# A selective scan with a gated MLP and a binary MLP on one core: loads of u and B on 64 rows, the second binary relu on ScalarE, one gating operation, last products in four steps

## The chip, the core and the metric

The kernel runs on one core of a Trainium2 chip. A core has five engines, each with an instruction stream of its own: PE (matrix products), DVE (vector), ACT (scalar, with function tables), POOL (general vector) and SP, which here only issues DMAs. They meet through semaphores. The metric is the device time of one execution in microseconds; lower is better.

## What is computed

Input x is 8 batches of 512 tokens of 128 numbers. It is normalised per token (layernorm), and the result `xn` goes through two blocks whose outputs are added to x:

```python
# block 1: E = 256, N = 64
xp = rmsnorm(xn) @ in_proj_W;  x_z, z = xp[..., :E], xp[..., E:]
xc = silu(depthwise_conv4(x_z) + conv_b)
dt = clip(softplus(xc @ dt_W + dt_b), 0.001, 0.1);  Bp = xc @ B_W;  Cp = xc @ C_W;  A = -exp(A_log)
def step(h, ins):                       # 512 steps in order, h is (8, 256, 64)
    h = exp(dt_t[..., None] * A) * h + dt_t[..., None] * B_t[:, None, :] * x_t[..., None]
    return h, einsum('ben,bn->be', h, C_t)
y = y * silu(z);  x = xn + y @ out_proj_W
x = x + (silu(n2 @ gate_W) * (n2 @ up_W)) @ down_W      # n2 = rmsnorm(x)
# block 2: weights of +1 and -1, layers 256 -> 512 -> 512 -> 128
h = s0 * conn(k0, [xn, -xn]);  h = relu(h) * 2;  h = s1 * conn(k1, h);  h = relu(h) * 2;  h = s2 * conn(k2, h)
```

## The kernel before

The work has two phases. In the first (up to about 175 us) the batches go one by one through norm, projection, convolution, softplus and the products for B and C. dt is written to `dt_stage` in DRAM in f32. u = dt times x is split into NP = 3 bf16 parts that add up to the f32 value and goes to `u_stage`, B likewise to `b_stage`. silu(z) stays in SBUF as `silu_z`. The core processes even and odd batches as two halves (bb) of the 128 partitions: a partition of the state is one pair (n, bb), a row of the state has Q = 4 batch pairs times E = 256 columns.

The second phase is the scan, 512 steps of t. Q is halved: two quarters are "self" (`state` in SBUF, decayed by POOL, added by DVE) and two are "acc" (held in PSUM, decayed by DVE, added by PE into PSUM). Per step:
- ACT turns a loaded dt row, broadcast over 64 partitions for each bb, into `decay` = exp(-A dt) (L1010, two steps at once) and copies the acc half to `state` (L1030);
- POOL multiplies `decay` and `state` for the two self quarters (L593, `decayed`);
- DVE multiplies the acc half in PSUM by `decay` (L1221) and adds POOL's product and PE's self input (L1232, two operations);
- PE forms the outer products of u and B: for acc L743, for self L750, each with contraction over 64 rows of `moving` (u parts) and `b_rows` (B parts); L798 contracts the state of three steps before (LAG) with C.

The rows of a product are the pairs of one u part and one B part of one batch. There are 3 x 3 x 4 = 36 for each of two hq, and they lie on the partitions `product_rows(hq)`, every third from 10 + hq on; the rest of the 128 partitions is zeroed once, by POOL and DVE (L578, L579, L1202, L1203). A chunk is TC = 16 steps. Its four loads are L194 (`load_u`, each u row broadcast to three partitions) and L201 (`load_b`), once for each hq.

SP issues, in the order of its program: dt loads (L392, two of 512 KB every two steps, one for each bb, each onto every second partition, as soon as the state of five slots before is done; `decay` has NDEC = 6 slots), the chunk loads half a body ahead, token loads and stores of results. All DMAs of the kernel are in one queue.

A body is STEPS = 32 steps (two chunks). The program has 3 bodies, then a loop of 4 rounds with 3 bodies each, then the last. Between its scan instructions each engine handles one group of 256 tokens of everything behind the scan (out projection, MLPs), by a table of step numbers K_...: at step k of a body come the group's entries k, k + 32 and k - 32, so that K_LAST = 33 means step 1 of the body after. The entries that matter here: K_GATED (DVE, steps 7 and 8, L1298: y times silu(z), two operations of 128 columns each), K_H2 (PE, the second binary layer, L883, steps 14 to 21 and 24 to 31), K_H2_RELU (DVE, its relus, L1345: 22 and 23 for the first half in two operations, 32 for the second), K_HID (33), K_LAST and LAST_STEPS (PE, L897, 12 products of the last binary layer and of down_W, shared over five steps 33 to 37) and K_XN_T (PE, transposes of the next group at step 2, L816). PE works in its own order, so what stands in front of the next L743 delays it, and L743 stands between two L1221 of DVE. After the scan the last group runs alone (`finish_last`).

## Time and profile before

| | us |
|---|---|
| runs of the kernel before | 1122.29, 1122.53, 1107.89 (median 1122.29) |
| the profiled execution, its own time | 1115.98 |
| its span from first to last instruction | 1114.2 |
| granted TensorE clock, mean | 0.96 |

A row of the page that groups instructions gives: line, engine, operation, out<-in with sizes, count, then busy time and mean ns of one, then the idle time of the engine before them and what ended it. In a view of stretches the columns are: stretch and length, busy time of each engine with the number of instructions, the granted clock, the mean busy share of the 16 DMA engines (DMA share) and GB/s. In a view of waits: who waited for what, us in total, times, the longest. In a timeline: start, duration, engine, line, operation, names, and in brackets idle time before it with its releaser.

### The profile page before, as it was taken

What the parts mean: (1) busy time and instruction counts of PE and PEld (TensorE: products, weight loads), DVE (VectorE), ACT (ScalarE), POOL (GpSimd) and SP (SyncE); (2) the same over time, 40 slices, a digit from 0 to 9 for tenths busy, and PEclk for the clock granted to TensorE, in tenths of its full rate; (3) what the DMA queues carried; (4) which work ended last, traced back from release to release, by engine and by line L of the source; (5) the groups of instructions that cost most, each with busy time, mean ns of one, the idle gap of its engine ahead of it and who ended that gap; (6) DMA issues with size and microseconds to landing.
All of it is one profiled execution on the core that took longest, in us unless ns stands there. A gap on an engine that the chain in (4) does not pass through costs nothing.

```text
span 1114.2 us, 27718 instructions
## 1 busy us (share of the span) xinstructions
PE 967.9 (87%) x8006; PEld 426.6 (38%) x8006; DVE 935.2 (84%) x2131; ACT 908.7 (82%) x1093; POOL 847.9 (76%) x1216
## 2 busy tenths in 40 slices
PE   5998883668999999998999887899998899999897
PEld 3555540113333343433333332334343334343436
DVE  5677663799989999997998887899998899999983
ACT  1666776789999999997988887899997899998980
POOL 6555513789888889887888786898887788988880
PEclk9999996789999999999999999899999899999999
...
GB/s 139 81 136 180 136 200 298 345 327 355 351 343 334 345 355 350 345 344 268 356 341 332 319 328 318 271 351 352 353 349 333 280 366 343 339 356 340 335 148 10
DMA packets 76758, 327.39 MB, mean 294 GB/s; under 512 B 13472, under 2 KB 32800, under 8 KB 41504
## 3 DMA queue, kind: packets, MB, share of 16 engines
...
HBM read 303.24 MB, written 22.02 MB: 292 GB/s over the span
## 4 chain that ended last, share of the span: by engine, by line
DVE 27%; PE 25%; POOL 19%; issue 16%; DMA 5%; ACT 5%; SPq 2%; DVEq 1%; POOLq 0%; ACTq 0%
POOL decayed L593 13%; DVE ps L1221 9%; PE ps L798 8%; DVE state L1232 7%; PE ps L743 5%; PE ps L897 5%; DMA decay<-dt_stage 4%; PE ps L883 3%; DVE h L1336 2%; ACT state L1030 2%; DVE h L1345 1%; DVE soft L1147 1%; POOL soft L543 1%; SPq L392 1%; POOL u_rest L553 1%
## 5 line engine op out<-in xcount | busy, mean ns | idle before, releaser
L593 POOL TENSOR_TENSOR decayed<-decay,state 128x256 f32<-128x256 f32 x1024 | 725.5, 733 | 169.1 <-DVE state L1232 125.4
L1010 ACT ACTIVATE decay<-decay,a_col 128x2048 f32<-128x2048 f32 x256 | 512.7, 2003 | 46.3 <-DMA decay<-dt_stage 36.5
L1232 DVE TENSOR_TENSOR state<-decayed,ps 128x256 f32<-128x256 f32 x1024 | 403.1, 417 | 55.4 <-POOL decayed L593 40.0
L1221 DVE TENSOR_TENSOR ps<-decay,ps 128x512 f32<-128x512 f32 x512 | 352.6, 689 | 40.5 <-ACT state L1030 17.2
L1030 ACT COPY state<-ps 128x512 f32<-128x512 f32 x512 | 288.9, 582 | 64.6 <-issue 43.2
L798 PE MATMUL ps<-state,c_cols 128*32 128x256 f32 x4096 | 338.2, 403 | 0.1
L743 PE MATMUL ps<-moving,b_rows 64*128 64x256 bf16 x1024 | 204.3, 281 | 100.5 <-DVE ps L1221 96.3
L750 PE MATMUL ps<-moving,b_rows 64*128 64x256 bf16 x1024 | 205.4, 282 | 12.0 <-DMA b_rows<-b_stage 12.0
L883 PE MATMUL ps<-h,w 128*128 128x256 f32 x512 | 175.8, 429 | 1.0 <-DVE h L1336 0.8
L743 PEld LDWEIGHTS ps<-moving,b_rows 64*128 64x128 bf16 x1024 | 58.4, 94 | 274.0 <-DVE ps L1221 172.3
L798 PEld LDWEIGHTS ps<-state,c_cols 128*32 128x32 f32 x4096 | 82.0, 109 | 113.4 <-issue 101.3
L883 PEld LDWEIGHTS ps<-h,w 128*128 128x128 f32 x512 | 79.7, 191 | 92.3 <-issue 89.1
L750 PEld LDWEIGHTS ps<-moving,b_rows 64*128 64x128 bf16 x1024 | 57.3, 95 | 12.4 <-DMA moving<-u_stage 12.3
L652 PE MATMUL ps<-n_feat,w_tap 128*128 128x512 f32 x128 | 59.3, 617 | 1.0 <-ACT n_feat L917 1.0
L897 PE MATMUL ps<-w,h 128*128 128x128 f32 x256 | 48.0, 305 | 1.0 <-DVE h L1345 1.0
L897 PEld LDWEIGHTS ps<-w,h 128*128 128x128 f32 x256 | 35.4, 196 | 26.2 <-issue 24.3
L848 PE MATMUL ps<-xn_feat,w 128*128 128x256 f32 x128 | 44.2, 429 | 0.2 <-DVE result L1354 0.2
L679 PE MATMUL ps<-w_dt,xc_feat 128*128 128x256 f32 x128 | 35.9, 439 | 9.0 <-ACT xc_feat L927 9.0
L679 PEld LDWEIGHTS ps<-w_dt,xc_feat 128*128 128x128 f32 x128 | 32.1, 328 | 12.9 <-ACT xc_feat L927 10.9
L652 PEld LDWEIGHTS ps<-n_feat,w_tap 128*128 128x128 f32 x128 | 24.8, 199 | 30.1 <-issue 30.1
L1147 DVE TENSOR_TENSOR soft<-soft 128x1024 f32<-128x1024 f32 x8 | 20.8, 2602 | 16.3 <-POOL soft L543 16.3
L543 POOL TENSOR_TENSOR soft<-soft 128x1024 f32<-128x1024 f32 x7 | 17.2, 2453 | 20.6 <-DVE soft L1136 20.6
...
## 6 DMA issues: line engine op xcount, KB each, us to landing
decay<-dt_stage SPq DMA_DIRECT2D x512, 512.0 KB, 6.6
moving<-u_stage SPq DMA_DIRECT2D x64, 288.0 KB
...
b_rows<-b_stage SPq DMA_DIRECT2D x64, 144.0 KB
dt_stage<-dt_tok SPq DMA_DIRECT2D x8, 512.0 KB, 3.1
u_stage<-u_parts SPq DMA_DIRECT2D x8, 512.0 KB, 2.8
x_tok<-in_L_attn_x_dram SPq DMA_DIRECT2D x4, 512.0 KB, 3.5
...
```

What stands on the lines that cost most here:

```text
L593: nc.gpsimd.tensor_tensor(decayed[:, p], decay[:, dec_slot(m, k), p, k % TS, :], state[:, (k - 1) % RING, p * E:(p + 1) * E], ALU.mult).th ...
L652: m = nc.tensor.matmul(ps[:, XC + h, :], w_tap[:, k, h * P:(h + 1) * P], n_feat[:, bass.ds(n, 1), k:k + T].rearrange("d o t -> d (o t)"), ...
L679: m = nc.tensor.matmul(ps[:, DTT + j // 2, (j % 2) * E:(j % 2 + 1) * E], xc_feat[:, bb, h, j:T:NJ], w_dt[:, h, :], start=(h == 0), stop=(h ...
L743: return nc.tensor.matmul(ps[:, acc_bank(m, k), p * E:(p + 1) * E], b_rows[rows(1), cb, p, kk, :], moving[rows(1), cb, kk, :], start=False ...
L750: return nc.tensor.matmul(ps[:, SELFP + k % 2, p * E:(p + 1) * E], b_rows[rows(0), cb, p, kk, :], moving[rows(0), cb, kk, :], start=True, ...
L798: m = nc.tensor.matmul(ps[q * 32:(q + 1) * 32, YP, 0:E], c_cols[:, cb, q, kk * 2 * TC:(kk + 1) * 2 * TC], state[:, k % RING, q * E:(q + 1) ...
L883: m = nc.tensor.matmul(ps[:, FB, c * GTOK:(c + 1) * GTOK], w1[:, n, f:f + P], h1[:, n, :], start=(n == 0), stop=(n == H1 // P - 1))
L897: m = nc.tensor.matmul(ps[:, FB, j * P:(j + 1) * P], terms[c][0][:, j * P:(j + 1) * P], terms[c][1], start=(c == 0), stop=(c == len(terms) ...
L1010: nc.scalar.activation(pair, pair, ACT.Exp, scale=a_col[:, 2:3]).then_inc(decay_ready, 1)
L1030: nc.scalar.copy(state[:, k % RING, SELF:QE], ps[:, acc_bank(m, k), :]).then_inc(acc_copied, 1)
L1221: nc.vector.tensor_tensor(ps[:, acc_bank(m, k), :].rearrange("p (q e) -> p q e", q=HQ), decay[:, dec_slot(m, k), HQ:Q, k % TS, :], ps[:, a ...
L1232: nc.vector.tensor_tensor(state[:, k % RING, p * E:(p + 1) * E], decayed[:, p], ps[:, SELFP + k % 2, p * E:(p + 1) * E], ALU.add).then_inc ...
```

## The change

It has five parts.
1. u and B get a fourth part of zeros (NS = 4), so there are 4 x 4 x 4 = 64 rows for each hq, and they lie on every second partition. The zero planes of `u_stage` and `b_stage` are written once by 24 stores of SP, from a part of `moving` that POOL has zeroed. The zeroing of the whole of `moving` goes.
2. The relu of the second binary layer moves from DVE to ACT, at steps 23 and 32, in one operation of 512 columns each.
3. `silu_z` is laid out by chunks, so that gating is one DVE operation of 512 columns at step 8.
4. K_LAST is 34 and LAST_STEPS is 4: the 12 products take steps 34 to 37, three a step.
5. A wait for the zero stores stands before the first chunk loads.

```diff
--- before.py
+++ after.py
-    ROWS = NP * NP * HALF
-    RSTEP = 3
-    RFIRST = HROW + RSTEP - 1 - RSTEP * (ROWS // 2)
-    assert RFIRST > 0 and HROW + HQ - 1 + RSTEP * (ROWS // 2) <= P
+    NS = NP + 1
+    ROWS = NS * NS * HALF
+    assert HQ * ROWS == P
...
-    u_stage = nc.dram_tensor("u_stage", (HQ, HQ, 2, NP, T, E), BF16, kind="Internal").ap()
+    u_stage = nc.dram_tensor("u_stage", (HQ, HQ, 2, NS, T, E), BF16, kind="Internal").ap()
     dt_stage = nc.dram_tensor("dt_stage", (2, T // TS, Q, TS, E), F32, kind="Internal").ap()
-    b_stage = nc.dram_tensor("b_stage", (HQ, HQ, 2, NP, NP, T, 2 * N), BF16, kind="Internal").ap()
+    b_stage = nc.dram_tensor("b_stage", (HQ, HQ, 2, NS, NS, T, 2 * N), BF16, kind="Internal").ap()
...
-        silu_z = sb("silu_z", [P, EH, B, T])
+        silu_z = sb("silu_z", [P, EH, NC, B, TC])
...
-            first = RFIRST - 2 + hq
-            return slice(first, first + RSTEP * (ROWS - 1) + 1, RSTEP)
+            return slice(hq, P, HQ)
 
         def load_u(sp, t, cb, hq):
 
             sp.dma_start(moving[product_rows(hq), cb].rearrange("r t e -> r (t e)"),
                          u_stage[hq, :, :, :, bass.ds(t, TC), :].rearrange("f b i t e -> (f b i) (t e)")
-                         .unsqueeze(1).broadcast_to([HALF * NP, NP, TC * E])
+                         .unsqueeze(1).broadcast_to([HALF * NS, NS, TC * E])
                          ).then_inc(chunk_loaded[cb], 16)
...
-        K_Y_T, K_GATED, K_OUT, K_X1, K_SQUARE, K_RRMS_SUM, K_RRMS, K_BASE, K_N2 = 6, (7, 8), 9, 11, 12, 13, 15, 12, 17
+        K_Y_T, K_GATED, K_OUT, K_X1, K_SQUARE, K_RRMS_SUM, K_RRMS, K_BASE, K_N2 = 6, 8, 9, 11, 12, 13, 15, 12, 17
         K_N2_T, K_N2_FEAT = 19, 20
         K_GATE, K_GATE_TANH, K_SILU, K_UP, K_HID = 22, 24, (25, 26), (30, 32), 33
         K_H1, K_H1_RELU = (7, 11), ((9, 10), (13,))
-        K_H2, K_H2_RELU = (14, 24), ((22, 23), (32,))
-        K_LAST, K_RESULT = 33, 38
-        H2_STEPS, LAST_STEPS = 8, 5
+        K_H2, K_H2_RELU = (14, 24), (23, 32)
+        K_LAST, K_RESULT = 34, 38
+        H2_STEPS, LAST_STEPS = 8, 4
...
+                def store_pads(n):
+
+                    q, bb = n // 2, n % 2
+                    u_rows, b_planes = u_stage[q % HQ, q // HQ, bb], b_stage[q % HQ, q // HQ, bb]
+                    zeros = moving[:, 1, 0:2 * NS].rearrange("p t e -> p (t e)")
+                    sp.dma_start(u_rows[NP].rearrange("(p j) e -> p (j e)", j=NJ),
+                                 zeros[:, 0:NJ * E]).then_inc(pads_stored, 16)
+                    sp.dma_start(b_planes[NP].rearrange("k (p j) n -> p k (j n)", j=NJ),
+                                 zeros[:, 0:NS * NJ * 2 * N].rearrange("p (k n) -> p k n", k=NS)).then_inc(pads_stored, 16)
+                    sp.dma_start(b_planes[0:NP, NP].rearrange("k (p j) n -> p k (j n)", j=NJ),
+                                 zeros[:, 0:NP * NJ * 2 * N].rearrange("p (k n) -> p k n", k=NP)).then_inc(pads_stored, 16)
...
+                sp.wait_ge(pad_zeroed, 1)
+                for n in range(B):
+                    store_pads(n)
...
                 sp.wait_ge(rows_zeroed, 2)
+                sp.wait_ge(pads_stored, 16 * PADS)
...
+                nc.gpsimd.memset(moving[:, 1, 0:2 * NS], 0.0).then_inc(pad_zeroed, 1)
...
-                    nc.gpsimd.memset(moving[:, 0], 0.0)
...
-                    nc.scalar.activation(silu_z[:, :, n, :], ps[:, ZB[n % 2]:ZB[n % 2] + EH, :], ACT.Silu
+                    nc.scalar.activation(silu_z[:, :, :, n, :], ps[:, ZB[n % 2]:ZB[n % 2] + EH, :]
+                                         .rearrange("p h (c t) -> p h c t", t=TC), ACT.Silu
                                          ).then_inc(S["z_ready"], 1)
...
+                    for r in range(2):
+                        if k == K_H2_RELU[r]:
+                            act.wait_ge(G["f_h2_proj"], g * 2 + r + 1)
+                            nc.scalar.activation(h2[:, 2 * r:2 * r + 2, :].rearrange("p c t -> p (c t)"), ps[:, FB, :],
+                                                 ACT.Relu, scale=s_fold[:, 0:1]).then_inc(G["f_h2_ready"], 1)
...
-                    nc.vector.memset(moving[:, 1], 0.0)
...
-                    if k in K_GATED:
-
-                        h = K_GATED.index(k)
-                        if h == 0:
-                            after(dve, "f_y_t_ready", g)
-                            after(dve, "f_proj_ready", g, back=1)
-                        for j in range(GT):
-                            m = nc.vector.tensor_tensor(
-                                gated[:, h, j * P:(j + 1) * P].rearrange("e (b t) -> e b t", b=B),
-                                ps[:, FA, (h * GT + j) * P:(h * GT + j + 1) * P]
-                                .rearrange("e (b t) -> e b t", b=B),
-                                silu_z[:, h, :, bass.ds(g * TG + j * TC, TC)], ALU.mult)
-                        if h == EH - 1:
-                            m.then_inc(G["f_gated_ready"], 1)
+                    if k == K_GATED:
+                        after(dve, "f_y_t_ready", g)
+                        after(dve, "f_proj_ready", g, back=1)
+                        nc.vector.tensor_tensor(
+                            gated[:], ps[:, FA, :].rearrange("e (h t) -> e h t", h=EH),
+                            silu_z[:, :, bass.ds(g * GT, GT)].rearrange("e h c b t -> e h (c b t)"), ALU.mult
+                        ).then_inc(G["f_gated_ready"], 1)
...
-                        if k in K_H2_RELU[r]:
-                            part = K_H2_RELU[r].index(k)
-                            if part == 0:
-                                dve.wait_ge(G["f_h2_proj"], g * 2 + r + 1)
-                            m = nc.vector.tensor_scalar(
-                                columns(h2[:, 2 * r:2 * r + 2, :].rearrange("p c t -> p (c t)"), part, K_H2_RELU[r]),
-                                columns(ps[:, FB, :], part, K_H2_RELU[r]), s_fold[:, 0:1], 0.0, ALU.mult, ALU.max)
-                            if k == K_H2_RELU[r][-1]:
-                                m.then_inc(G["f_h2_ready"], 1)
```

The lines of the changed kernel are numbered a little higher: L1243 is L1221, L1254 is L1232, L760 and L767 are L743 and L750, L815 is L798, L914 is L897, L833 is L816.

On DVE, around steps 21 to 25 of the second body, before. L1345 writes `h` (the relu), L1318 is the first half of the silu at step 25.

```order
L1221 TENSOR_TENSOR ps<-decay,ps 128x512
L1232 TENSOR_TENSOR state<-decayed,ps 128x256 x2
L1345 TENSOR_SCALAR h<-ps,s_fold 128x256
L1221 TENSOR_TENSOR ps<-decay,ps 128x512
L1232 TENSOR_TENSOR state<-decayed,ps 128x256 x2
L1345 TENSOR_SCALAR h<-ps,s_fold 128x256
L1221 TENSOR_TENSOR ps<-decay,ps 128x512
L1232 TENSOR_TENSOR state<-decayed,ps 128x256 x2
L1221 TENSOR_TENSOR ps<-decay,ps 128x512
L1232 TENSOR_TENSOR state<-decayed,ps 128x256 x2
L1318 SCALAR_TENSOR_TENSOR gate<-gate,ps 128x256
```

And in the changed kernel:

```order
L1243 TENSOR_TENSOR ps<-decay,ps 128x512
L1254 TENSOR_TENSOR state<-decayed,ps 128x256 x2
L1243 TENSOR_TENSOR ps<-decay,ps 128x512
L1254 TENSOR_TENSOR state<-decayed,ps 128x256 x2
L1243 TENSOR_TENSOR ps<-decay,ps 128x512
L1254 TENSOR_TENSOR state<-decayed,ps 128x256 x2
L1243 TENSOR_TENSOR ps<-decay,ps 128x512
L1254 TENSOR_TENSOR state<-decayed,ps 128x256 x2
L1333 SCALAR_TENSOR_TENSOR gate<-gate,ps 128x256
```

The two relus between the steps are gone; the scan's own operations stand as they did.

On PE, steps 1 and 2 of the third body, before. L743 and L750 alternate for the acc and self products, L798 contracts, L897 is the last products, L816 transposes the next group's `xn`.

```order
L750 MATMUL ps<-moving,b_rows 128x256
L743 MATMUL ps<-moving,b_rows 128x256
L750 MATMUL ps<-moving,b_rows 128x256
L798 MATMUL ps<-state,c_cols 32x256 x4
L897 MATMUL ps<-w,h 128x128 x2
L743 MATMUL ps<-moving,b_rows 128x256
L750 MATMUL ps<-moving,b_rows 128x256
L743 MATMUL ps<-moving,b_rows 128x256
L750 MATMUL ps<-moving,b_rows 128x256
L798 MATMUL ps<-state,c_cols 32x256 x4
L897 MATMUL ps<-w,h 128x128 x2
L816 MATMUL ps<-ident,xn 128x128 x2
```

And in the changed kernel:

```order
L767 MATMUL ps<-moving,b_rows 128x256
L760 MATMUL ps<-moving,b_rows 128x256
L767 MATMUL ps<-moving,b_rows 128x256
L815 MATMUL ps<-state,c_cols 32x256 x4
L760 MATMUL ps<-moving,b_rows 128x256
L767 MATMUL ps<-moving,b_rows 128x256
L760 MATMUL ps<-moving,b_rows 128x256
L767 MATMUL ps<-moving,b_rows 128x256
L815 MATMUL ps<-state,c_cols 32x256 x4
L914 MATMUL ps<-w,h 128x128 x3
L833 MATMUL ps<-ident,xn 128x128 x2
```

Step 1 has no last product any more; step 2 has three of them, and the transposes behind them.

On DVE, steps 6 to 8 of the third body, before. L1298 is the gating.

```order
L1221 TENSOR_TENSOR ps<-decay,ps 128x512
L1232 TENSOR_TENSOR state<-decayed,ps 128x256 x2
L1298 TENSOR_TENSOR gated<-ps,silu_z 128x128 x2
L1221 TENSOR_TENSOR ps<-decay,ps 128x512
L1232 TENSOR_TENSOR state<-decayed,ps 128x256 x2
L1298 TENSOR_TENSOR gated<-ps,silu_z 128x128 x2
L1221 TENSOR_TENSOR ps<-decay,ps 128x512
```

And in the changed kernel:

```order
L1243 TENSOR_TENSOR ps<-decay,ps 128x512
L1254 TENSOR_TENSOR state<-decayed,ps 128x256 x2
L1243 TENSOR_TENSOR ps<-decay,ps 128x512
L1254 TENSOR_TENSOR state<-decayed,ps 128x256 x2
L1316 TENSOR_TENSOR gated<-ps,silu_z 128x512
L1243 TENSOR_TENSOR ps<-decay,ps 128x512
L1254 TENSOR_TENSOR state<-decayed,ps 128x256 x2
```

Between steps 7 and 8 nothing is left, and one operation of 512 columns stands behind step 8.

## Rows read from the trace of the kernel before

**Rows 1.** The page: busy time of the engines; GB/s in 40 slices of 27.9 us.
```profile
PE 967.9 (87%) x8006; PEld 426.6 (38%) x8006; DVE 935.2 (84%) x2131; ACT 908.7 (82%) x1093; POOL 847.9 (76%) x1216
...
GB/s 139 81 136 180 136 200 298 345 327 355 351 343 334 345 355 350 345 344 268 356 341 332 319 328 318 271 351 352 353 349 333 280 366 343 339 356 340 335 148 10
```
**Rows 2.** Stretches from body to body, L1221 alone: length, DVE busy, clock, DMA share, GB/s.
```profile
352.10:406.10 54.00, 21.99 (x33) 1.00 1.00 350
...
574.80:633.50 58.70, 22.08 (x32) 0.94 0.99 330
633.50:695.80 62.30, 22.09 (x32) 0.97 0.97 319
...
806.90:866.20 59.30, 22.02 (x32) 0.99 0.98 340
...
175.00:242.70 67.70, 22.04 (x32) 0.70 0.93 329
...
sum 855.20, DVE 330.52; mean DVE 22.03
```
**Rows 3.** Stretches of one microsecond, all engines; the last two numbers are DMA share, GB/s.
```profile
392.00:393.00 1.00, 1.00 (x12) 0.46 (x10) 1.00 (x3) 0.68 (x2) 0.94 (x2) 1.00 1.06 246
393.00:394.00 1.00, 0.94 (x14) 0.27 (x12) 1.00 (x4) 0.62 (x2) 0.76 (x2) 1.00 1.05 250
...
398.00:399.00 1.00, 0.85 (x6) 0.26 (x6) 1.00 (x4) 1.00 (x2) 0.88 (x3) 1.00 1.03 434
```
**Rows 4.** Waits of L1010 for dt: all; from 526 to 693 us; from 175 to 242.
```profile
  DMA decay<-dt_stage: 36.5, 22
```
```profile
ACT decay L1010 <- DMA decay<-dt_stage: 15.9, 13, 2.7
```
```profile
ACT decay L1010 <- DMA decay<-dt_stage: 14.6, 2, 10.5
```
**Rows 5.** The page, DMA issues: name, count, KB of one, us to landing.
```profile
decay<-dt_stage SPq DMA_DIRECT2D x512, 512.0 KB, 6.6
moving<-u_stage SPq DMA_DIRECT2D x64, 288.0 KB
...
b_rows<-b_stage SPq DMA_DIRECT2D x64, 144.0 KB
```
**Rows 6.** The chain that ended last, a piece of the first phase: start, us, what.
```profile
23.40 1.76 DVE moving L1202
```
**Rows 7.** Groups of instructions, forms kept apart.
```profile
L1221 DVE TENSOR_TENSOR ps<-decay,ps 128x512 f32<-128x512 f32 x512 | 352.6, 689 | 40.5 <-ACT state L1030 17.2 <-ACT decay L1010 13.6 <-PE ps L743 5.4
...
L1298 DVE TENSOR_TENSOR gated<-ps,silu_z 128x128 f32<-128x128 f32 x64 | 15.3, 281 | 0.0
L1345 DVE TENSOR_SCALAR h<-ps,s_fold 128x256 f32<-128x256 f32 x32 | 15.2, 479 | 0.8 <-PE ps L883 0.8
...
L1345 DVE TENSOR_SCALAR h<-ps,s_fold 128x512 f32<-128x512 f32 x16 | 11.9, 745 | 2.9 <-PE ps L883 2.9
...
L1071 ACT ACTIVATE gate<-ps 128x512 f32<-128x512 f32 x16 | 9.6, 602 | 3.6 <-PE ps L861 3.6
```
**Rows 8.** Timeline of POOL, then of ACT, around steps 22 to 25 of an undisturbed body.
```profile
792.81 1.42 POOL L593 TENSOR_TENSOR decayed<-decay,state 128x256 f32<-128x256 f32 x2 [0.47 <-DVE state L1232]
794.46 2.12 POOL L593 TENSOR_TENSOR decayed<-decay,state 128x256 f32<-128x256 f32 x3 [0.23 <-DVE state L1232]
```
```profile
794.14 0.59 ACT L1030 COPY state<-ps 128x512 f32<-128x512 f32 x1 [0.70 <-issue]
```
**Rows 9.** Timeline of PE, the first product of steps 2 to 5 of that body.
```profile
757.49 0.28 PE L743 MATMUL ps<-moving,b_rows 64*128 64x256 bf16 x1 [0.26 <-DVE ps L1221]
...
759.24 0.28 PE L743 MATMUL ps<-moving,b_rows 64*128 64x256 bf16 x1
...
761.00 0.28 PE L743 MATMUL ps<-moving,b_rows 64*128 64x256 bf16 x1
...
762.54 0.28 PE L743 MATMUL ps<-moving,b_rows 64*128 64x256 bf16 x1
```

3 lines of the change are left out of this document (added).

## The prediction

> **What bounds the kernel now.** I read the shares of the engines first, then one stretch per body of the scan, then the DMA, and last the steps one by one. The shares [rows 1] name no single engine: PE, DVE, ACT and POOL are busy 87, 84, 82 and 76% of the span. So averages don't decide, and the scan is read body by body (32 steps each, 16 bodies). The stretches from one body's first L1221 to the next one's [rows 2] fall into two kinds. Undisturbed ones last 54.0 us, 1.69 us a step (the one from 352.1 stands for five): there the step recurrence (POOL decays, DVE adds, PE multiplies, ACT copies and exponentiates) sets the pace and not the data. The others last 55 to 68 us. The 15 stretches sum to 855.2 us; 15 times 54.0 is 810.0, so 45.2 us are lost in the disturbed ones.
>
> What disturbs those? In the undisturbed stretch the DMA share is already 1.00 at 350 GB/s [rows 2]. In the stretch from 574.8 the share is 0.99 and only 330 GB/s are moved; it takes 58.7 us. So a full DMA moves now more, now less. Within microseconds the difference is larger [rows 3]: 246 and 250 GB/s while loads of u and B are being worked off, 434 when dt alone is moving, with the share at 1.03 to 1.06 in all three. ACT waits for dt in total 36.5 us, 14.6 of them in the first body and 15.9 between 526 and 693 us [rows 4]. Stretches such as the one from 806.9 (59.3 us) contain a pause of all engines at the edge of the loop (three bodies per round); in the one from 633.5 both kinds meet (62.3 us). The change doesn't touch the loop.
>
> **The loads.** A chunk of 16 steps brings 16 dt loads of 512 KB and two each of u (288 KB) and B (144 KB) [rows 5], together 9056 KB. Padding NP=3 to NS=4 makes u 512 KB (64 rows of 8 KB for 36) and B 256 KB, so a chunk is 9728 KB, 7.4% more. At 27.0 us a chunk that asks for 369 GB/s, above the 350 at which the share is 1.00 now, and below the 434 of dt alone. All depends on whether u and B keep slowing the rest. The new rows are every second partition, hq to 127, the very pattern of a dt load; the old ones were every third from 10 to 116. I take it that the slow microseconds come from that mismatch, because the slow time is longer than the u and B bytes need (432 KB at 434 GB/s are 1.0 us, and the rows show two at 250) and the rate is back at 434 five microseconds later with dt loads as before. If the mismatch goes, the chunk needs 9.96 MB / 0.43 = 23 us of DMA, under the 27.0 there are.
> The Trainium skill, "DMA: Bandwidth & Descriptors", section "Why a DMA increments its semaphore by 16 and not by 1", says that a transfer uses the largest count up to 16 that divides the outer size on both sides. By it the loads of 36 rows run on 12 engines and those of 64 on all 16. The page "SBUF — State Buffer", section on the DMA port swizzle, gives each four partitions a port, by which old u rows and dt rows meet on ports in an irregular order and new ones don't. By the two the busiest engine goes from 584 to 608 KB a chunk, 4.1% and not 7.4%. No row here shows single engines.
>
> What that is worth: of the 45.2 us, the stretch from 574.8 lost 4.7, the one from 633.5 lost 8.3, of which 5.3 go with the loop edge as in the one from 806.9, so 3.0, and the stretches behind edges some 2 more. That is 9.5 us of waiting for data outside the start; I take 8 as gained. Bounds: nothing that remains of it is below 0 (gain 9.5), and the loss if u and B slow the DMA in proportion to their bytes is the first rival's.
> At the start of the scan the first two chunks bring 1344 KB more and the dt loads queue behind them (67.7 us for the first body, at 329 GB/s). At that rate it is +4.2 us; if the rate rises to 350 the whole 24 MB of that body take no longer than before. I take +1.5, ends -1 and +4.2.
>
> **Work before the scan.** The zeroing of moving on DVE goes: 1.76 us, and it stands on the chain that ended last [rows 6]. That is -1.8. POOL's zeroing ran beside it; its short new one of 2048 columns comes ahead of anything POOL is asked for: 0. Added are 24 stores of zeros, 9.4 MB, on SP before the first store of results. They hide in slices 2 and 3, where only 81 and 136 GB/s move [rows 1]: at 350 there is room for (269+214) x 27.9 us = 13 MB. SP's own next work, the first store of results, waits for DVE's first dt. Without that cover they would cost up to 27 us, late; I count 0.
>
> **The steps.** DVE loses per body two relus of 256 columns and one of 512 (478, 478 and 745 ns), and four gatings of 281 ns (15.3 us for 64, so 0.24 each) become one of 512 columns, for which L1221 is the nearest row, 689 ns [rows 7]. DVE's work falls by 1.70 + 0.96 - 0.69 = 2.0 us a body, 31 us in all, if DVE alone decided. It doesn't, so I follow the places.
> - Steps 22 and 23: POOL waits 0.47 us for DVE at 792.81 and 0.23 at 794.46, right behind the two relus [rows 8]. Both waits go, apart from semaphore time: -0.6 us. ACT takes the relu at step 23, where it idles 0.70 us ahead of its copy at 794.14 [rows 8]; a 512-column ACT operation is 602 ns [rows 7]. It fits. The relu waits for PE's products of step 21, over a step earlier; behind it in ACT's order stand the exponential for steps 26 and 27, which POOL and DVE need two steps later, and the copies of 22 and 23. So 0 for ACT, and 0.25 a body if it were late.
> - Step 0 (32 of the group before): the 745 ns relu leaves DVE. With it DVE has about 1.93 us in that step (0.60, 0.67 and 0.66 for L1221, two L1232 and the relu, each started 0.1 before the last one's end), and POOL 1.53: it is worth 0.4. But the last products now start one step later and take steps 2 to 5, three a step, where they took steps 1 to 5 with 2, 2, 3, 2, 3. PE is without a gap there: its steps 2 to 5 start at 757.49, 759.24, 761.00 and 762.54 [rows 9]: 1.76 us with three products, 1.54 with two. Steps 2 and 4 get a third product, 2 x 0.22. So +0.45 against -0.4: 0. Only the 0.26 us gap before 757.49 was free.
> - Gating: step 7 gets 0.4 shorter, step 8 by 0.2 longer, and POOL paces both. I take +0.1, bounds -0.2 and +0.3.
> Per body -0.5, taken for 15 bodies: -7. Ends: -31 (DVE's whole relief) and +4 (that, with nothing gained).
> After the scan DVE's and ACT's operations stand in a row with PE: 478 x 2 and 745 become two ACT operations of 602, gating saves 0.2: -0.7.
>
> **Sum.** The profiled execution took 1115.98 us: -1.8 + 1.5 - 8 - 7 - 0.7 = -16, so 1100. The median of the runs is 1122.3 and the lowest 1107.9, which is about the profiled execution without its 8 us of data waits; against the median it is -2.0%, against the profiled one -1.4%. A measurement of this kernel can tell about 2% from no change.
>
> **Rivals.**
> 1. The DMA becomes the bound (slower). Place: every chunk. If a full DMA moves no more than the 350 GB/s of today, 9.96 MB take 28.5 us for 27.0: +1.5 x 32 = 48 us, and the 8 of waits are inside it. 1116 + 48 - 8 - 2.5 (the work before and after the scan) = 1153; no step gain then shows. It decides as soon as the mean rate at full share stays under 369 GB/s. For it: share 1.00 already. Against: 434 in clean microseconds, and undisturbed bodies that never wait for dt. Half of it, by a rate of 359, is about 1129.
> By the skill's count of engines above, only 4.1% is added to the busiest one: 28.1 us a chunk, +35 us, 1141.
> 2. DVE's relief counts in full, since it lags POOL at many steps: -25 for -7, and clean data: 1116 - 1.8 + 1.5 - 9.5 - 25 - 0.7 = 1080. Against: steps without any DVE filler already last POOL's two operations, 1.42 us [rows 8] of the 1.69, and POOL waits little behind them.
> 3. Nothing moves: the slow microseconds are the memory's own, unchanged by the shape, and PE takes the step gain back: 1116 - 2.5 + 1.5 = 1115, with a little of the waits 1114.
>
> **Chances.** Forecast (1092 to 1108) 0.50, rival 1 0.13 with its half cases, rival 2 0.16, rival 3 0.21. The forecast lies on the 2% line of the median, so a good third of it counts as faster: 0.20 + 0.16 = 0.36 faster; slower 0.12; the rest within 2%, 0.52. The range leaves out the full rival 1 and a tail of rival 2: 1082 to 1134.
>
> **What would show it.** Right: stretches of the windows view at DMA share below 0.97 with over 365 GB/s; no microsecond under 300; ACT's wait for dt outside the first body near 0; undisturbed bodies of 53.5 us; POOL's waits behind steps 22 and 23 gone, PE still without gap in steps 2 to 6; the first body no longer than 70 us. Wrong: share 1.00 in bodies of 56 us and more with ACT waiting for dt in each (rival 1); bodies near 52.3 (rival 2); bodies of 54.1 with the same disturbed ones (rival 3); or a start of the scan later than now, which would put the zero stores on the path.

## The result, and the profile after

The changed kernel takes 1181.09 us (median of 4 runs, 1171.59 to 1185.36) against 1122.41 for the one before: a ratio of 1.0557, 95% interval 1.0426 to 1.0687. The ratio compares means and leaves out one slow run of the kernel before (1129.42 us). It was forecast at 1100, with a range to 1134. So it is slower by 5.6%, and further out than any rival went.

First the page of the changed kernel, the busy time of its engines and the GB/s in 40 slices (29.6 us each), as [rows 1]:

```profile
PE 990.3 (84%) x8006; PEld 429.0 (36%) x8006; DVE 918.6 (78%) x2034; ACT 925.3 (78%) x1125; POOL 846.2 (72%) x1216
...
GB/s 280 273 160 115 166 255 371 359 334 340 348 347 339 351 336 333 300 331 296 340 335 326 330 338 283 337 353 343 312 357 314 312 332 343 327 339 337 334 194 10
```
All engines are less busy as a share, and the DMA moves no more per second in the scan than before, though it has 7.4% more to bring. The stretches from body to body (length, L1243 busy, clock, DMA share, GB/s), as [rows 2], say where the time is; L1243 is the L1221 of before:

```profile
172.90:242.30 69.40, 22.03 (x32) 0.64 0.99 351
...
360.10:419.70 59.60, 22.13 (x33) 0.97 0.97 338
...
480.40:547.50 67.10, 22.10 (x33) 0.97 0.99 322
...
735.70:792.50 56.80, 22.02 (x33) 0.94 0.96 325
...
sum 927.90, DVE 331.20; mean DVE 22.08
```
```profile
1100.80:1154.60 53.80, 21.41 (x32) 0.97 0.70 253
```
The 15 stretches sum to 927.9 us for 855.2: +72.7, which is more than the whole loss of the profiled execution (span 1183.5 for 1114.2, +69.3). None of the 15 is an undisturbed one any more. The only body that runs at its own pace is the last, 53.8 us: it loads one more chunk and not two, and its last dt load is issued 17 us before it ends, so the DMA share is 0.70. The scan begins at 172.9 us, 2.1 earlier than before, and what follows it is 1.0 shorter (from the last L1243 at 1155.2 to the end 28.3 us, for 29.3). So the loss lies in the scan alone, in the 15 bodies before the last.

The waits (engine, line, what for: us in total, times, longest), as [rows 4]:

```profile
POOL decayed L610 <- DVE state L1254: 199.4, 288, 7.6
...
ACT decay L1028 <- DMA decay<-dt_stage: 122.0, 76, 10.7
...
DVE ps L1243 <- ACT state L1048: 89.7, 78, 4.8
```
ACT's wait for dt is 122.0 us for 36.5, POOL's for DVE 199.4 for 125.4, DVE's for ACT's copies 89.7 for 17.2. The other two are mostly the echo of the first, as a timeline of ACT, then of DVE, in the body from 360.1 shows (start, length, what, [idle before, releaser]):

```profile
404.24 0.64 ACT L1094 ACTIVATE gate<-ps 128x512 f32<-128x512 f32 x1
407.88 2.00 ACT L1028 ACTIVATE decay<-decay,a_col 128x2048 f32<-128x2048 f32 x1 [3.00 <-DMA decay<-dt_stage]
409.78 1.05 ACT L1048 COPY state<-ps 128x512 f32<-128x512 f32 x2
```
```profile
410.45 0.69 DVE L1243 TENSOR_TENSOR ps<-decay,ps 128x512 f32<-128x512 f32 x1 [2.64 <-ACT state L1048]
```
The exponential waits 3.00 us for its dt, ACT's copies of the steps at hand stand behind it in ACT's order, DVE waits 2.64 us for those copies, and POOL for DVE. One late dt load stops the whole recurrence. Something comes on top of the waits: the granted clock in the bodies after the first is 0.87 to 0.97, where the undisturbed ones before had 0.99 and 1.00, and PE's contraction takes 418 ns for 403. No run separates that part. And why is dt late? One-us stretches of all engines, as [rows 3] (last two numbers: DMA share, GB/s), and the DMA issues with their us to landing, as [rows 5]:

```profile
395.00:396.00 1.00, 1.00 (x13) 0.59 (x12) 1.00 (x3) 1.00 (x1) 0.69 (x2) 1.00 0.89 180
396.00:397.00 1.00, 1.00 (x15) 0.31 (x13) 0.82 (x3) 1.00 (x3) 1.00 (x3) 1.00 1.06 205
...
398.00:399.00 1.00, 0.76 (x12) 0.27 (x12) 1.00 (x4) 1.00 (x1) 0.52 (x2) 1.00 1.03 434
```
```profile
decay<-dt_stage SPq DMA_DIRECT2D x512, 512.0 KB, 9.7
moving<-u_stage SPq DMA_DIRECT2D x64, 512.0 KB, 12.5
b_rows<-b_stage SPq DMA_DIRECT2D x64, 256.0 KB, 12.3
```
While u and B are worked off the rate is 180 and 205 GB/s, lower than the 246 and 250 of before, at a share that is about full; with dt alone it is 434 again. The start of the scan shows the same loads almost by themselves. The first four are issued from 172.3 to 174.8 us, and eight of dt only behind them, in the same queue. Up to 180 us 1.53 MB are moved, which is about what the four loads bring (1.57 MB), and then the rate jumps:

```profile
175.00:176.00 1.00, 0.00 (x0) 0.50 1.00 250
176.00:177.00 1.00, 0.00 (x0) 0.50 0.94 238
177.00:178.00 1.00, 0.00 (x0) 0.50 1.24 307
178.00:179.00 1.00, 0.00 (x0) 0.50 0.94 221
179.00:180.00 1.00, 0.00 (x0) 0.50 0.85 205
...
182.00:183.00 1.00, 0.85 (x2) 0.50 1.01 426
```
(Stretches with POOL's busy time only.) The loads of u and B are slow here too, 244 GB/s in the mean of the first five, though by the bytes no dt moves beside them yet. So it is a property of these loads, not of their meeting dt loads, which is what the prediction had supposed.

### The profile page after: what moved, and what is told of

Its sections match the earlier page's. It is cut to its first block and busy times, and to the rows that moved or that the text cites. A ratio compares the mean times of both kernels' runs of the same rounds, so it can differ in the third digit from the quotient of the medians.

```text
span 1183.5 us, 27658 instructions
## 1 busy us (share of the span) xinstructions
PE 990.3 (84%) x8006; PEld 429.0 (36%) x8006; DVE 918.6 (78%) x2034; ACT 925.3 (78%) x1125; POOL 846.2 (72%) x1216
## 5 line engine op out<-in xcount | busy, mean ns | idle before, releaser
L610 POOL TENSOR_TENSOR decayed<-decay,state 128x256 f32<-128x256 f32 x1024 | 725.3, 733 | 239.0 <-DVE state L1254 199.4
L1028 ACT ACTIVATE decay<-decay,a_col 128x2048 f32<-128x2048 f32 x256 | 513.5, 2006 | 128.5 <-DMA decay<-dt_stage 122.0
L1243 DVE TENSOR_TENSOR ps<-decay,ps 128x512 f32<-128x512 f32 x512 | 353.3, 690 | 123.4 <-ACT state L1048 89.7
L1254 DVE TENSOR_TENSOR state<-decayed,ps 128x256 f32<-128x256 f32 x1024 | 401.5, 416 | 55.0 <-POOL decayed L610 23.6
L815 PE MATMUL ps<-state,c_cols 128*32 128x256 f32 x4096 | 352.3, 418 | 0.0
L760 PE MATMUL ps<-moving,b_rows 64*128 64x256 bf16 x1024 | 211.5, 289 | 144.3 <-DVE ps L1243 140.7
L1048 ACT COPY state<-ps 128x512 f32<-128x512 f32 x512 | 280.6, 584 | 40.0 <-issue 18.4
L767 PE MATMUL ps<-moving,b_rows 64*128 64x256 bf16 x1024 | 212.6, 290 | 13.6 <-DMA b_rows<-b_stage 13.6
L900 PE MATMUL ps<-h,w 128*128 128x256 f32 x512 | 184.8, 448 | 0.8 <-DVE h L1351 0.8
L760 PEld LDWEIGHTS ps<-moving,b_rows 64*128 64x128 bf16 x1024 | 58.7, 95 | 330.2 <-DVE ps L1243 210.3
L815 PEld LDWEIGHTS ps<-state,c_cols 128*32 128x32 f32 x4096 | 83.7, 111 | 119.9 <-issue 107.3
L900 PEld LDWEIGHTS ps<-h,w 128*128 128x128 f32 x512 | 83.6, 200 | 100.6 <-issue 97.6
L767 PEld LDWEIGHTS ps<-moving,b_rows 64*128 64x128 bf16 x1024 | 58.0, 96 | 14.0 <-DMA moving<-u_stage 13.9
L914 PE MATMUL ps<-w,h 128*128 128x128 f32 x256 | 44.6, 299 | 0.3 <-ACT h L1088 0.3
L914 PEld LDWEIGHTS ps<-w,h 128*128 128x128 f32 x256 | 33.5, 191 | 25.1 <-issue 24.3
L696 PE MATMUL ps<-w_dt,xc_feat 128*128 128x256 f32 x128 | 32.8, 410 | 10.0 <-ACT xc_feat L944 10.0
L561 POOL TENSOR_TENSOR soft<-soft 128x1024 f32<-128x1024 f32 x7 | 17.2, 2451 | 20.9 <-DVE soft L1159 20.9
```

What stands on the lines that cost most here:

```text
L610: nc.gpsimd.tensor_tensor(decayed[:, p], decay[:, dec_slot(m, k), p, k % TS, :], state[:, (k - 1) % RING, p * E:(p + 1) * E], ALU.mult).th ...
L696: m = nc.tensor.matmul(ps[:, DTT + j // 2, (j % 2) * E:(j % 2 + 1) * E], xc_feat[:, bb, h, j:T:NJ], w_dt[:, h, :], start=(h == 0), stop=(h ...
L760: return nc.tensor.matmul(ps[:, acc_bank(m, k), p * E:(p + 1) * E], b_rows[rows(1), cb, p, kk, :], moving[rows(1), cb, kk, :], start=False ...
L767: return nc.tensor.matmul(ps[:, SELFP + k % 2, p * E:(p + 1) * E], b_rows[rows(0), cb, p, kk, :], moving[rows(0), cb, kk, :], start=True, ...
L815: m = nc.tensor.matmul(ps[q * 32:(q + 1) * 32, YP, 0:E], c_cols[:, cb, q, kk * 2 * TC:(kk + 1) * 2 * TC], state[:, k % RING, q * E:(q + 1) ...
L900: m = nc.tensor.matmul(ps[:, FB, c * GTOK:(c + 1) * GTOK], w1[:, n, f:f + P], h1[:, n, :], start=(n == 0), stop=(n == H1 // P - 1))
```

## The experiments

**Halves of the change.** First the rest alone (ReLU on ScalarE, single gating, last products in four steps), with the loads of before:

```diff
 # the kernel before + the edits at L951 (layout of silu_z), L1088, L1316 and K_LAST; load_u, load_b, NP=3 as before
```


> The kernel before with parts 2 to 4 of the change alone: the relu on ACT, one gating operation, last products in four steps; the loads of u and B stay on 36 rows. Theory A (the loads alone cost the time): the time of before or up to 8 us less, 1112 to 1122, ratio 0.99 to 1.00; undisturbed bodies of 53.5 us, ACT's wait for dt about 36 us as before. Rival B (ACT is now too full, and its relu ahead of the exponential delays the copies): 1140 or more, with DVE waiting for ACT's copies as in the changed kernel (89.7 us).

Measured 1116.86 us, ratio 0.9994 (0.9955 to 1.0032). Its wait for dt and its undisturbed body (windows, all engines):

```profile
ACT decay L1011 <- DMA decay<-dt_stage: 32.8, 23, 9.4
```
```profile
349.10:402.70 53.60, 49.91 (x476) 20.69 (x472) 49.57 (x115) 51.04 (x64) 47.47 (x71) 1.00 0.97 350
```
The body is 53.6 us for 54.0, as forecast within 0.1; in the whole time nothing can be seen of it.

Then the loads alone:

```diff
 # the kernel before + NS = NP + 1, 64 rows for u and B, zero stores; all else as before
```


> The kernel before with part 1 alone: u and B padded to 64 rows on every second partition, with the zero stores. Theory A: the whole loss, 1175 to 1190 us, ACT waiting 100 us or more for dt. Rival B: no more than 1140. The first phase is seen too: if the zero stores cost time, the first decay exponential starts later than at 170.9 us.

Measured 1180.58 us, ratio 1.0543 (1.0492 to 1.0593), wait for dt 118.2 us. The whole loss is the loads'.

**Is it the pitch of the rows?** The pitch is the distance in DRAM from one row that a load reads to the next.

```diff
-    u_stage = nc.dram_tensor("u_stage", (HQ, HQ, 2, NS, T, E), ...).ap()
+    u_stage = nc.dram_tensor("u_stage", (HQ, HQ, 2, NS, T + TC, E), ...).ap()[:, :, :, :, 0:T]
 # b_stage likewise
```


> The changed kernel with the token dimension of the two staging tensors in DRAM made 16 tokens longer, so that rows of u lie 264 KB apart for 256 and rows of B 132 KB for 128. Nothing else moves. Theory C (16 engines read at a power-of-two pitch and meet in the same part of the memory): the microseconds of u and B loads rise from 180 to 250 GB/s to over 350, ACT's wait for dt falls below 40 us, and the time to 1095 to 1115. Rival D (the destination, or the number of bytes, sets it): 1170 to 1190, the slow microseconds as they are.

1171.96 us, ratio 1.0481 (1.0417 to 1.0546), wait for dt 107.9 us. Of the 88 us that lie between the change and the fastest kernels below, that is some 9, and the intervals of this run and of the loads alone overlap.

**One source row for all 64 partitions.** This keeps destination, bytes and issues, but the products are other ones, since every partition gets the same u and B:

```diff
-    u_stage[hq, :, :, :, bass.ds(t, TC), :]...unsqueeze(1).broadcast_to([HALF * NS, NS, TC * E])
+    u_stage[hq, 0:1, 0, 0, bass.ds(t, TC), :]...broadcast_to([ROWS, TC * E])
 # load_b likewise
```


> The changed kernel with each load of u and of B reading one single row of its staging tensor for all 64 partitions, as a dt load does; what is multiplied is then not the products of the reference's u and B. Destination, bytes and issue stay. Theory C and every theory in which the source is at fault: 427 GB/s in all microseconds at full share, body stretches of about 53.5 us but for the loop's edges, 1090 to 1105. Rival D (destination or bytes): 1170 to 1190, since the writes are the same.

1093.19 us, ratio 0.9774 (0.9723 to 0.9824). A body:

```profile
347.30:400.90 53.60, 49.91 (x476) 20.68 (x472) 49.59 (x115) 51.02 (x64) 47.48 (x71) 1.00 0.99 377
```
The same bytes, at 377 GB/s, wait for nothing. So 7.4% more bytes, the first rival's ground, cost nothing here, and the time is 23 us under before. I then took the source rows' place for the cause, wrongly, as the next two show.

**The place of the rows.** Staging tensors laid out by chunk, with the 64-row loads and with the 36-row loads of before:

```diff
-    u_stage = nc.dram_tensor("u_stage", (HQ, HQ, 2, NS, T, E), ...)
+    u_stage = nc.dram_tensor("u_stage", (HQ, NC, HQ, 2, NS, TC, E), ...)
```


> The staging tensors of the changed kernel are laid out by chunk, so that the rows of one chunk load lie in one unbroken block (u 16 rows of 8 KB = 128 KB, B 64 rows of 4 KB = 256 KB); shapes of destination, bytes and instructions of the scan are those of the changed kernel. Theory E (the place of the source rows is at fault: 64 rows of B 256 KB apart, 16 of u 512 KB apart): the loads run at 350 GB/s or more even at their start, ScalarE waits for dt 12 to 40 us in all, the body without a loop edge takes 53.6 us, time 1093 to 1115. Rival F (each byte that is read for the first time is slow whatever its place; one row passed because it was read once and then again): one-us stretches of the chunk loads stay at 180 to 270 GB/s, time 1165 to 1185.

(The distances named there are twice too large: u's rows are 256 KB apart and B's 128 KB.)

> The same layout by chunk, under the kernel before's loads of 36 rows on 12 queue engines, with the ReLU on ScalarE and the single gating. Theory E: the slow microseconds of the kernel before (246 and 250 GB/s) are of the same cause, so they go; ScalarE's wait for dt falls from 32.8 us to about 12, and the time from 1117 to 1093 to 1105. Rival F: no change, 1112 to 1120. A second rival: with 12 of 16 engines on these loads the slowness is that of fewer engines, which the layout leaves: 1108 to 1120.

1183.13 us, ratio 1.0564 (1.0508 to 1.0620), and 1113.64 us, ratio 0.9975 (0.9935 to 1.0014). Nothing moved. The theory of scattered rows fell.

**Which of the two loads?** One source row for u alone, then for B alone (again other products):

> The changed kernel, where each chunk load of u alone reads one row for all 64 partitions (so it computes other products), B as in the change. If u's scattered rows of 8 KB (each read by four partitions) are at fault: time near 1093 to 1110. If B's 64 distinct rows are: 1160 to 1180. By bytes read for the first time (u 128 KB of 384 KB distinct per half chunk) a third of the loss of 88 us would go: about 1152.

> The counterpart: each chunk load of B alone reads one row for all 64 partitions (other products), u as in the change. If B's scattered rows are at fault: 1093 to 1110. If u's are: 1160 to 1180. By distinct bytes two thirds of the loss would go: about 1122.

1091.51 us, ratio 0.9753 (0.9699 to 0.9808), and 1176.58 us, ratio 1.0514 (1.0456 to 1.0571). Their waits:

```profile
ACT decay L1028 <- DMA decay<-dt_stage: 12.2, 2, 9.6
```
```profile
ACT decay L1029 <- DMA decay<-dt_stage: 110.8, 67, 10.1
```
It is the load of u alone; B's 64 different rows are harmless.

**What of u's load?** It differs from B's in three things: packets of 8 KB, a source that repeats each row, and a pattern of two outer dimensions (16 x 4). Four edits followed:

```diff
 # four loads of 16 plain rows      # 64 different pieces, shape 16 x 4 (other products)
+ for k in range(NS): load 16 rows  + u_stage[hq, ..., 0:NS * TC, :] "f b i (k t) e -> (f b i) k (t e)"
 # one token more per row           # two loads of half the tokens
+ (HQ, HQ, 2, NS, T + 1, E)         + for h in range(2): 16 x 4 rows of 4 KB
```


> The changed kernel, where each chunk load of u is issued as four loads of 16 plain rows (one for each of the four copies) instead of one load whose source repeats every row four times; same bytes to the same partitions, same products. Theory G (the repeat inside the load is at fault: four neighbouring partitions ask for the same 8 KB at the same time): 350 GB/s or more in the chunk loads, ScalarE waits for dt about 12 us, time 1090 to 1110. Rival H (16 different rows of 8 KB read at one time are slow, however they are asked for): 1165 to 1185, one-us stretches of 180 to 270 GB/s stay. More issues on SP (256 of u instead of 64) may cost some us at the loop's edges in either case.

1189.07 us, ratio 1.0627 (1.0537 to 1.0718). With 256 issues of u instead of 64 this run mixes two things and settles little by itself. Its load, 16 plain rows to partitions 8 apart, comes again in the third series below and is slow there too.

> The changed kernel, where each chunk load of u has the same shape (16 x 4 x 8 KB) but the four copies are read from four following pieces of 8 KB of each row instead of from one (so it computes other products, from the first tokens). Theory G (the repeat): no repeat, so 350 GB/s and more, time 1090 to 1110. Rival H (different rows of 8 KB): now 64 different ones, 1170 or more. Rival J (the shape 16 x 4 and how it is dealt out to the 16 queue engines): 1170 to 1185, like the changed kernel.

1184.21 us, ratio 1.0605 (1.0494 to 1.0716): slow without any repeat, as the shape's rival (and the one of different rows) had it.

> The changed kernel with one token (512 B) more in each row of u's staging tensor: the 16 rows that a load reads then start 512 B further each, modulo 8 KB, where in every version so far (plain, padded by 8 KB, laid out by chunk) all 16 starts are multiples of 8 KB. Theory K (queue engines in step on different rows at the same offset modulo 8 KB meet at the same part of the memory; one row is one address and doesn't): 350 GB/s or more in the chunk loads, ScalarE waits about 12 us for dt, time 1090 to 1110. Rival L (different rows in 8 KB packets are slow at any offset): 1170 to 1190, ScalarE's wait for dt stays at 110 to 125 us.

1179.18 us, ratio 1.0527 (1.0437 to 1.0617): not the offset either.

> The changed kernel with each chunk load of u issued as two loads of half the tokens, so its rows are of 4 KB, as those of B (whose 64 different rows ran at full rate in the run with one row for u). Rival L with the packet's size as the cause: 1090 to 1115. Theory K and every theory by place, offset or number of different bytes: 1170 to 1190, as the starts stay in step.

1156.61 us, ratio 1.0333 (1.0206 to 1.0461): smaller packets in the same shape win a part back; no theory had named that value.

**Kinds of load by themselves.** To tell shape, rows and the running scan apart, a series of loads was put behind the end of the changed kernel, each kind four loads, waited for before the next:

```diff
+ for n, load in enumerate(series * 2):
+     for cb in range(2):
+         for hq in range(HQ):
+             load(cb, hq).then_inc(probed, 16)
+     sp.wait_ge(probed, 64 * (n + 1))
```


> The changed kernel with a series of loads behind its end, when nothing else runs: 13 kinds, each four loads into the buffers of u (or B), waited for before the next kind, and the whole twice; so its time is 1181 plus some 150 to 250 us of series. Kinds: 8 KB rows, 64 partitions: (1) one row x 64 copies; (2) 2 rows x 32; (3) 4 x 16; (4) 8 x 8; (5) 16 x 4, the load of the change; (6) the 16 rows with the copies as the outer dimension; (7) 4 rows with copies outer; (8) 64 different pieces in the shape 16 x 4; (9) 64 different rows at one pitch; (10) as 5 to 64 neighbouring partitions; 4 KB rows: (11) one row x 64; (12) 16 x 4; (13) B's 64 rows. Theory H (different 8 KB rows at one time): 1 fast (2 MB in about 5 to 6 us), 2 to 4 in between and growing, 5 to 10 slow (8 to 9 us), 12 slow in part, 11 and 13 fast (1 MB in about 3 to 4 us). Rival J (the shape with an inner dimension of copies, and how it is dealt out to the queue engines): 1, 9, 11, 13 fast, 2 to 5, 8, 10, 12 slow. Rival M (it takes the running scan, such as its own accesses to on-chip memory, for the loads to be slow): all fast here.

The whole took 1556.8 us, 376 more than without the series. Stretches inside seven kinds, in the order 1 (one row x 64), 2 (2 x 32), 3 (4 x 16), 4 (8 x 8), 5 (16 x 4, the change), 8 (64 pieces as 16 x 4) and 9 (64 rows at one pitch); the last two numbers are DMA share and GB/s:

```profile
1370.00:1376.00 6.00, 0.00 (x0) 0.50 0.89 322
1190.00:1229.00 39.00, 0.00 (x0) 0.50 0.13 53
1232.00:1252.00 20.00, 0.00 (x0) 0.50 0.25 102
1255.00:1270.00 15.00, 0.00 (x0) 0.50 0.50 134
1273.00:1281.00 8.00, 0.00 (x0) 0.50 0.98 237
...
1321.00:1329.00 8.00, 0.00 (x0) 0.50 0.99 239
1332.00:1337.00 5.00, 0.00 (x0) 0.50 0.96 341
```
Two things stand here. The share of the 16 DMA engines (queue engines in the recorded texts) at work is 0.13, 0.25 and 0.50 for outer dimensions of 2, 4 and 8, so 2, 4 and 8 engines: the outer dimension sets their number. The Trainium skill, "DMA: Bandwidth & Descriptors", "Why a DMA increments its semaphore by 16 and not by 1", says that a load runs on the largest number of engines up to 16 that divides the slowest dimension of both sides; the shares agree. And with an outer dimension of 16, where all engines are at work (0.98), they move 237 GB/s, while 64 rows in one dimension move 341 with nothing else changed. Different rows are not the cause (kind 9 is fast with 64 of them), nor the repeat (kind 8 is slow without), nor the scan (none is running). By the packets' times in the trace, a median packet of 8 KB took 555 ns in kind 5 and 309 in kind 9. The rival of the shape is right.

> A second series of 13 kinds of load behind the end of the changed kernel, four loads each, twice: (1) 64 rows at one pitch; (2) 16 x 4, the change; (3) 32 x 2; (4) 32 rows; (5) 16 rows at a pitch of 8 KB, (6) the 16 rows of u; (7) 12 x 3, the load of u of the kernel before; (8) 36 rows; (9) 16 x 3; (10) 48 rows; (11) 36 rows of 4 KB; (12) 16 x 4 of 2 KB; (13) 64 rows of 2 KB. If the slowness comes of copies behind an outer dimension of 16: packets of 2, 3?, 7, 9 slow (about 555 ns against 309), 1, 4, 5, 6, 8, 10 at 309. If outer dimensions below 16 leave engines idle as in the first series (2 x 32: 52 GB/s, 4 x 16: 98): 7 on 12 engines, and 8 and 11 show whether 36 rows at one pitch use 12 too.

Kinds 2 (16 x 4), 3 (32 x 2), 7 (12 x 3, the u load of before) and 8 (36 rows at one pitch):

```profile
1188.50:1196.50 8.00, 0.00 (x0) 0.50 0.99 239
1200.00:1205.50 5.50, 0.00 (x0) 0.50 0.95 346
...
1225.00:1230.00 5.00, 0.00 (x0) 0.50 0.72 223
1233.00:1238.00 5.00, 0.00 (x0) 0.50 0.72 215
```
32 x 2 is as fast as 64 rows, so copies as such are no burden. The 36-row loads work on 0.72 of the engines, which fits 12 of 16, in either shape; here they filled partitions 0 to 71 only, not the spread ones of the kernel before. Not as expected: 32 rows to partitions 0 to 63 ran at 206 GB/s with all engines busy, though in one dimension. That led to the third series.

> A third series of loads of 8 KB rows behind the end of the changed kernel, on how rows and partitions meet: to 64 neighbouring partitions (1) 64 rows at one pitch, (2) 32 x 2, (3) 16 x 4; (4) one row to 32 partitions 2 apart, (5) to 32 partitions 4 apart; (6) 32 rows and (7) 16 x 2 to partitions 4 apart, (8) 16 x 2 to partitions 2 apart; (9) 16 rows to partitions 8 apart, (10) 2 apart; (11), (12) one row likewise; (13) the change's 16 x 4. If the source's shape alone sets the pace, 4 and 5, 6, 9 to 12 go by it at either distance of the partitions and 1 and 2 are fast. If it is which partitions the queue engines write to at one time, 1 and 2 are slow too, or 5, 6, 9 and 11 differ from their neighbours 4, 10 and 12.

Kinds 1 (64 rows to 64 neighbouring partitions), 2 (32 x 2 to the same), 4 (one row to 32 partitions 2 apart, so within 64) and 5 (one row to 32 partitions 4 apart, so over all 128), then 6 and 7 (to the same partitions as 5, 32 rows at one pitch and 16 x 2):

```profile
1173.00:1181.00 8.00, 0.00 (x0) 0.50 1.03 228
1185.00:1193.00 8.00, 0.00 (x0) 0.50 1.02 219
...
1209.00:1213.00 4.00, 0.00 (x0) 0.50 1.02 211
1216.50:1220.00 3.50, 0.00 (x0) 0.50 0.75 251
1222.50:1226.00 3.50, 0.00 (x0) 0.50 0.76 260
1228.50:1232.00 3.50, 0.00 (x0) 0.50 0.88 269
```
The two shapes that were fast to every second partition are slow to one half of the partitions, and one single row is slow to partitions 2 apart (211 at a share of 1.02, which is 207 per full share) and fast to partitions 4 apart (251 at 0.75, or 335). So it is the writing side that is slow: which partitions the engines write at one time. The Trainium skill, "SBUF — State Buffer", "Door 1: The DMA port swizzle", says that partitions 0 to 63 reach only 8 of 16 ports and gives about 218 GB/s for them; the 211 to 228 here agree roughly.

That leaves 16 x 4 over all 128 partitions, at 237 and 239 GB/s and, in this third series, at 256. It moves little more than a load that reaches half of the partitions. The copies are not needed for that. 16 plain rows to partitions 8 apart, over all 128 as well, took 476 and 494 ns a packet in the two passes (kind 9), and one row to the same 16 partitions 522 and 462 (kind 11), where 32 rows to partitions 4 apart took 309. And 16 x 2 to the partitions that 32 rows fill at 260 GB/s with a share of 0.76 (342 for a full share) reached 269 at 0.88 (306). So what is shown is that an outer dimension of 16 is slower than one of 32 or 64 to the same partitions, whatever is read.

The reason is my reading, argued and not shown: with 16 outer rows each engine gets four partitions in a row (0, 2, 4, 6 for the first, 8 to 14 for the second), and engines in step then write to the same half of the ports, whereas with 32 or 64 outer rows the rows are dealt out so that they spread. No row shows a single engine, so this stays open.

**The fast shape in the kernel.** A load of 64 rows at one pitch needs u stored four times; 32 x 2 needs it twice.

```diff
-    u_stage = nc.dram_tensor("u_stage", (HQ, HQ, 2, NS, T, E), ...)
+    u_stage = nc.dram_tensor("u_stage", (HQ, HQ, 2, NS, COPIES, T, E), ...)
-    ... .unsqueeze(1).broadcast_to([HALF * NS, NS, TC * E])
+    ... .unsqueeze(1).broadcast_to([HALF * NS * COPIES, NS // COPIES, TC * E])
 # and each store of u, and of its zeros, issued COPIES times
```


> The changed kernel with u stored four times, so that a chunk load of u reads 64 rows at one pitch (the shape of kind 9 in the series: 316 and 311 GB/s over four loads with their start, against 224 and 220 for the change's 16 x 4). Theory J (the shape decides): slow one-us stretches go, ScalarE's wait for dt falls from 122 to about 12 us, the scan takes 916 us or less as with one source row; against that 18 MB more of stores and 6 MB more of zeros ahead of the scan, which start it 0 to 20 us later: time 1093 to 1115, slowest where the stores aren't hidden 1130. Rival H (different rows of 8 KB are slow when the scan runs, whatever the shape): 1180 to 1200.

1109.47 us, ratio 0.9962 (0.9928 to 0.9996). The scan takes 892 us (188.0 to 1080.2) for the change's 982, but begins 15 us later.

> The kernel before's 36-row loads with u stored three times (36 rows at one pitch), and the ReLU on ScalarE and the single gating. Theory J: the loads run without slow stretches but still on few queue engines; ScalarE's wait for dt falls from 32.8 us to about 12 to 20, time 1095 to 1115, the more so as fewer bytes are loaded than with 64 rows; 12 MB more of stores ahead of the scan. Rival H: 1115 to 1130.

With 36 rows (three copies) 1114.46 us, ratio 0.9977 (0.9924 to 1.0030), wait for dt 31.2 us: the one pitch does not help there, as kinds 7 and 8 say.

> The changed kernel with u stored twice and the chunk load of u in the shape 32 x 2 (324 and 308 GB/s in the second series, as 64 rows at one pitch, against 221 and 222 for 16 x 4). With four copies the scan took 891.5 us instead of 982.3 but began at 188.0 instead of 172.9 us; twice the stores instead of four times should begin it at 174 to 180. Theory J: time 1094 to 1104, the fastest of all that compute the reference's result. Rival H: 1170 or more.

1095.02 us (median of 6, 1091.38 to 1097.45), ratio 0.9846 (0.9800 to 0.9892). Its GB/s on the page, wait for dt, a stretch without and one with a loop edge:

```profile
GB/s 267 367 209 239 161 253 337 403 348 382 358 366 376 369 384 375 381 367 340 345 379 377 381 375 367 316 391 369 367 382 354 322 379 374 383 375 380 373 146 11
```
```profile
ACT decay L1031 <- DMA decay<-dt_stage: 13.5, 2, 10.7
```
```profile
349.50:403.20 53.70, 50.04 (x476) 20.68 (x472) 49.71 (x116) 51.13 (x64) 47.52 (x71) 1.00 0.99 377
...
623.90:681.70 57.80, 51.07 (x482) 20.99 (x474) 49.77 (x116) 51.59 (x65) 47.32 (x71) 1.00 0.97 376
```
The scan begins at 175.6 us and takes 890 us. This version beats both: 1.5% or some 17 us under the kernel before, with an interval clear of 1, and 86 us under the change. It brings the same bytes to the same partitions as the change; only the pattern of u's source differs (and 6 MB more of u and 2 MB of zeros are stored ahead of the scan, which starts 2.7 us later than the change's).

## Why the prediction was wrong, and where it was right

**The step that failed** is "I take it that the slow microseconds come from that mismatch", priced at -8. The loads by themselves made the kernel 5.4% slower instead. The fact behind it was right: loads of u and B slow the DMA, and this costs the kernel before some 20 us of waits for dt (32.8 and 36.5 us, against 12.1 to 13.5 with one source row or two copies of u, and 20.5 with four copies). The cause was not. The new rows do lie as dt's do, but it also matters how a load's rows are divided among the 16 engines: dt and B have 64 rows in one dimension, u has 16 x 4, and that ran at 237 GB/s for 341. From before to after the rate in the slow microseconds fell (246 and 250 to 180 and 205) rather than rose. I had looked at which partitions a load fills and at its bytes, and never at how its two outer dimensions are divided. It spread to B behind it as well: in the scan of the changed kernel a median packet of B (4 KB) took 278 ns, and 275 with one row for B (1176.58 us), but 159 once u alone read one row.

The size can be estimated. A body brings 16.8 MB of dt and 3.15 MB of u and B. At the 434 GB/s of dt alone and some 213 (the mean of the 221 and 205 above), that is 38.7 + 14.8 = 53.5 us of full DMA; at 244, the mean of the five microseconds from 175 to 180, it is 38.7 + 12.9 = 51.6 us. The steps take 53.6 us, so 0 to 2 us of slack are left, and most of each wait and loop edge would be lost for good. With u and B at 350 it is 38.7 + 9.0 = 47.7 us, 6 us of slack. The estimate is not the whole of it: the same sum for the kernel before (1.77 MB of u and B at 248) gives 45.8 us, and dt came late there too. The DMA share doesn't show slack either, as it is 0.99 in the fast bodies at 377 GB/s. The measured loss is 72.7 us over 15 stretches, 4.8 each.

**Rival 1** had the right place and the right point of decision (a mean rate at full share under 369 GB/s; it is 315 to 351) and the wrong reason: more bytes. At those bytes 376 and 377 GB/s are moved, and the bodies are undisturbed but for the loop's edges. Its 1153 took the rate of before, 350, as the worst; the change lowered it. A rate that is read from a mix is not a bound for another mix. The cited rule on dividing engines was right (0.72 for 36 rows), but the 4.1% worked out by it counted bytes per engine, not what an engine's packet takes.

**Term by term.** Before the scan -1.8: the scan began 2.1 us earlier, and the stores of zeros cost nothing; right. Start of the scan +1.5: the first body went from 67.7 to 69.4, so +1.7, but by luck: with the fast shape it takes 64.6 with the same bytes, and with the loads of before and the rest of the change 65.3. Steps -7: the body went from 54.0 to 53.6 us where it can be seen, 0.4 for the forecast 0.5. Both of POOL's waits at steps 22 and 23 went. The timeline of POOL, first before and then in the version with two copies:

```profile
789.54 2.81 POOL L593 TENSOR_TENSOR decayed<-decay,state 128x256 f32<-128x256 f32 x4 [0.47 <-DVE state L1232]
```
```profile
386.48 7.24 POOL L613 TENSOR_TENSOR decayed<-decay,state 128x256 f32<-128x256 f32 x10 [0.47 <-DVE state L1257]
```
The 0.47 here is the wait two steps earlier, behind DVE's `n_feat`, which the change doesn't touch. In both kernels it comes some 37 us after the body's first L1221 or its like. Behind it the 0.47 and the 0.23 of [rows 8] are gone: ten operations without a gap. From this wait to the body's end it is 16.7 us for 17.4, the forecast -0.6. The stretch before it grew by 0.2 us, for the forecast +0.1 of gating and last products. So both terms came near their forecast. The sizes of the new operations, in the changed kernel:

```profile
L1088 ACT ACTIVATE h<-ps,s_fold 128x512 f32<-128x512 f32 x32 | 22.4, 700 | 6.9 <-PE ps L900 6.9
...
L1316 DVE TENSOR_TENSOR gated<-ps,silu_z 128x512 f32<-128x512 f32 x16 | 10.9, 683 | 0.0
```
The gating is 683 ns for the 689 taken; the ReLU on ACT is 700 for 602, which is hidden. The operations that left and came make 31.5 us less of work for DVE by their rows (15.2 + 11.9 + 15.3 - 10.9), as forecast, and DVE's busy time on the page fell from 935.2 to 918.6. Bodies of 53.6 us show that DVE's relief does not count in full, so the second rival was wrong. After the scan -0.7: it is 1.0 shorter. In the whole time of the rest alone the step gain doesn't show (0.9994, 0.9955 to 1.0032): about 6 us of 1116 is 0.5%, just outside that interval. That the waits for dt swallow part of it is likely and not shown.
